# Row maxima of an attention block in two bf16 parts, stacked by two transfers of one partition each

## The reference

```python
x = x + layernorm(attn(layernorm(x), wq, wk, wv, wo))
x = x + layernorm(ffn(layernorm(x), W_base, b_base, W_gate, A, B))

# attn
scores = einsum('bqhd,bkhd->bhqk', q, k) / sqrt(HEAD_DIM)     # q, k after rotary embedding
scores = scores + mask                                        # causal
attn = softmax(scores, axis=-1)
out = einsum('bhqk,bkhd->bqhd', attn, v).reshape(bsz, seq_len, 512)
return out @ wo
```

## Time and profile before

| | us |
|---|---|
| three runs: median | 265.6 |
| lowest, highest | 265.14, 267.56 |
| profiled execution, its own time | 264.58 |
| its span, first to last instruction | 262.9 |
| mean granted clock of TensorE | 0.95 of 2.4 GHz |
| busy: TensorE matmul | 208.9 |
| busy: VectorE | 173.1 |
| busy: ScalarE | 136.1 |
| busy: POOL | 117.8 |

### The profile page before, as it was taken

The page is one execution under the profiler, slowest core; times in us unless marked ns, Lnnn a source line. Parts: engine busy times, 40 slices in busy tenths (PEclk is TensorE's granted clock), DMA queues, the critical chain, the costliest instruction groups (busy, mean ns, idle before and its releaser), DMA issues.

```text
span 262.9 us, 3819 instructions
## 1 busy us (share of the span) xinstructions
PE 208.9 (79%) x1291; PEld 128.0 (49%) x1304; DVE 173.1 (66%) x414; ACT 136.1 (52%) x238; POOL 117.8 (45%) x93
## 2 busy tenths in 40 slices
PE   0799999876764999959994999699479888997860
PEld 0666534343432544434541544144379667886750
DVE  1974257776958567726773673346178988988874
ACT  2432503330343767747845664673085384778672
POOL 8001425522293666736827533881544253222132
PEclk9999999999998699968999799999979999999995
DMA  6993379779920607749066304033420001101113
GB/s 201 368 385 146 104 209 216 236 258 193 280 73 4 150 6 244 152 84 191 12 125 115 82 9 87 1 62 71 82 55 30 2 0 41 40 2 40 40 41 120
DMA packets 33962, 29.95 MB, mean 114 GB/s; under 512 B 3736, under 2 KB 29464, under 8 KB 33944
## 3 DMA queue, kind: packets, MB, share of 16 engines
q1 hardware_dynamic: 33944, 29.72, 42.4%
HBM read 17.19 MB, written 10.09 MB: 104 GB/s over the span
## 4 chain that ended last, share of the span: by engine, by line
PE 26%; DVE 18%; SPq 17%; DMA 16%; issue 11%; POOL 5%; ACT 4%; POOLq 1%; DVEq 0%; ACTq 0%
DMA region_b<-mrow 7%; SPq L364 5%; SPq L366 4%; PE ps L1082 4%; DVE stats L739 3%; PE ps L997 3%; PE ps L1056 3%; PE ps L973 3%; SPq L308 3%; PE ps L987 3%; DMA region_b<-q_scr 2%; DMA rden_bc<-r_scr 2%; PE ps L1145 2%; SPq L324 2%; POOL region_b L495 2%
## 5 line engine op out<-in xcount | busy, mean ns | idle before, releaser
L913 DVE TENSOR_REDUCE nmax<-ps 128x4 f32<-128x1024 f32 x32 | 39.1, 1223 | 25.7 <-PE ps L1056 25.7
L508 POOL TENSOR_SCALAR_AFFINE_SELECT region_a<-region_a 128x1024 f32<-128x1024 f32 x32 | 35.2, 1108 | 24.5 <-ACT region_a L685 24.4
L1082 PE MATMUL ps<-region_b,kst 99*128 99x512 bf16 x96 | 30.0, 420 | 10.5 <-DMA region_b<-mrow 9.2
L685 ACT ACTIVATE region_a<-ps 128x1024 f32<-128x1024 f32 x32 | 32.7, 1021 | 1.9 <-PE ps L1082 1.9
L682 ACT ACTIVATE region_a<-ps 128x512 f32<-128x512 f32 x32 | 19.2, 598 | 22.0 <-PE ps L1082 21.4
L987 PE MATMUL ps<-region_a,region_c 128*128 128x512 f32 x64 | 29.0, 598 | 0.0
L910 DVE TENSOR_REDUCE nmax<-ps 128x4 f32<-128x512 f32 x32 | 21.8, 683 | 9.4 <-PE ps L1040 9.3
L1097 PE MATMUL ps<-region_a,v_aug 128*32 128x512 f32 x192 | 25.2, 603 | 1.7 <-POOL region_a L508 1.7
L550 ACT ACTIVATE std<-mv,eps_sb 128x1 f32<-128x1 f32 x32 | 9.4, 293 | 32.6 <-DVE mv L740 32.6
L1056 PEld LDWEIGHTS ps<-kst,region_b 96*128 96x128 bf16 x256 | 18.9, 105 | 7.8 <-issue 2.8
L544 ACT ACT_TABLE_LOAD x17 | 21.8, 1283 | 1.1 <-PEq L1242 0.8
(11 more groups left out here) (107 smaller groups left out, 422.7 us busy)
## 6 DMA issues: line engine op xcount, KB each, us to landing
region_b<-q_scr SPq DMA_DIRECT2D x8, 768.0 KB, 6.9
q_scr<-region_c SPq DMA_DIRECT2D x8, 384.0 KB, 3.5
x_sb<-x SPq DMA_DIRECT2D x8, 256.0 KB, 5.4
q_scr<-region_c SPq DMA_DIRECT2D x8, 256.0 KB, 3.4
attn_t<-o_sb SPq DMA_DIRECT2D x32, 64.0 KB, 2.3
rden_bc<-r_scr SPq DMA_DIRECT2D x8, 256.0 KB, 3.3
out<-region_b SPq DMA_DIRECT2D x8, 256.0 KB, 2.0
kst<-k_scr SPq DMA_DIRECT2D x8, 192.0 KB, 3.3
```

The costliest lines, as they stand in the source:

```text
L508: pool.affine_select(out=blocks, in_=blocks, compare_op=ALU.is_ge, fill=0.0, base=0, pattern=[[0, 2], [0, REP], [1, P]], channel_multiplie ...
L685: nc.scalar.activation(probs[:, u % PRING, 1:3, :], ps[:, 4:6, :], ACT.Exp, scale=float(HEAD_DIM) ** -0.5).then_inc(exp_done, 1)
L913: nc.vector.tensor_reduce(nmax[:, gi % 2, 1, heads], ps[:, 1:3, :].rearrange("p a (r k) -> p r a k", r=REP), AX.XY, ALU.max, negate=True). ...
L1082: last = nc.tensor.matmul(ps[:, 3 + j, :], kst[0:TROWS, slot, k, kt * P:(kt + 1) * P], qst[0:TROWS, slot, k * REP:(k + 1) * REP, qt * P:(q ...
```

## The change

The maxima go in two bf16 parts: a cast to bf16, and a subtraction whose result is written as bf16. The third part, its cast and its subtraction are left out, and with them the tile `nmax_r`. The contraction of L1082 has 98 rows where it had 99. The stack is issued as two transfers, each from 16 partitions of `mrow` to one partition of `qst`; both add to the same semaphore, and the waits for it count 32 per group where they counted 16. In the new file the stack's issue is L353, the cast L925 and the subtraction L926; the lines of SP behind it are two further down.

```diff
+MAX_PARTS = 2
...
-TROWS = SROWS + PARTS
+TROWS = SROWS + MAX_PARTS
...
-        nmax_r = sb("nmax_r", [P, 2, 2, GROUP_HEADS])
-        nmax_p = sb("nmax_p", [P, 2, PARTS, GROUP_HEADS], BF16)
+        nmax_p = sb("nmax_p", [P, 2, MAX_PARTS, GROUP_HEADS], BF16)
...
             def stack_max(gi):
                 sp.wait_ge(mrow_ready, gi + 1)
-                sp.dma_start(qst[SROWS:TROWS, gi % RING, :, :], mrow[0:PARTS * GROUP_HEADS, gi % 2, :])\
-                    .then_inc(mrow_stacked[gi % 2], 16)
+                for part in range(MAX_PARTS):
+                    sp.dma_start(qst[SROWS + part:SROWS + part + 1, gi % RING, :, :],
+                                 mrow[part * GROUP_HEADS:(part + 1) * GROUP_HEADS, gi % 2, :])\
+                        .then_inc(mrow_stacked[gi % 2], 16)
...
                     if gi >= 2:
-                        act.wait_ge(mrow_stacked[gi % 2], 16 * (gi // 2))
-                    nc.scalar.copy(mrow[0:PARTS * GROUP_HEADS, gi % 2, :],
-                                   ps[0:PARTS * GROUP_HEADS, 0, 0:P].bitcast(BF16)).then_inc(mrow_ready, 1)
+                        act.wait_ge(mrow_stacked[gi % 2], 16 * MAX_PARTS * (gi // 2))
+                    nc.scalar.copy(mrow[0:MAX_PARTS * GROUP_HEADS, gi % 2, :],
+                                   ps[0:MAX_PARTS * GROUP_HEADS, 0, 0:P].bitcast(BF16)).then_inc(mrow_ready, 1)
...
-                    full, left = nmax[:, (gi - 1) % 2, :, :], nmax_r[:, (gi - 1) % 2, :, :]
-                    high, mid, low = (nmax_p[:, :, j, :] for j in range(PARTS))
+                    full = nmax[:, (gi - 1) % 2, :, :]
+                    high, low = (nmax_p[:, :, j, :] for j in range(MAX_PARTS))
...
                     link(nc.vector.tensor_copy(high, full))
-                    link(nc.vector.tensor_tensor(left, full, high, ALU.subtract))
-                    link(nc.vector.tensor_copy(mid, left))
-                    nc.vector.tensor_tensor(low, left, mid, ALU.subtract).then_inc(nmax_split, 1)
+                    nc.vector.tensor_tensor(low, full, high, ALU.subtract).then_inc(nmax_split, 1)
...
-                    last = nc.tensor.transpose(ps[0:PARTS * GROUP_HEADS, 0, qt * 64:(qt + 1) * 64].bitcast(BF16),
+                    last = nc.tensor.transpose(ps[0:MAX_PARTS * GROUP_HEADS, 0, qt * 64:(qt + 1) * 64].bitcast(BF16),
...
-                    pe.wait_ge(mrow_stacked[gi % 2], 16 * (gi // 2 + 1))
+                    pe.wait_ge(mrow_stacked[gi % 2], 16 * MAX_PARTS * (gi // 2 + 1))
```

## The result

Over 20 executions of each, the changed kernel took 266.00 us in the median (263.30 to 267.13) and the kernel before 265.76 (262.25 to 269.63). The ratio is 1.010, with a 95% interval of 1.0059 to 1.014. Two repetitions gave 1.0024 and 1.0025. So the forecast of 265.8 us is within 0.2 us of both means, but a ratio of 1.010 would put the changed kernel at 268.3.

A forecast was written before the change was run, and what follows sets the result against it. It looked to the attention stage, where the row maxima's stack transfer held 7% of the span, the chain's largest entry. Terms -0.3 + 0.45 - 0.4 + 0.5 = +0.25 us gave 265.8 us by the median, range 263.4 to 267.8.

The forecast's parts named there:

- Part 1: VectorE's split: dropping a cast and a subtraction saves 0.42 us per group, on the path only in group 1; -0.3 us.
- Part 3: The stack's spread over DMA engines, 16 instead of 3, shifts its landing: -0.4 us in group 3, +0.5 in group 5.
- Part 2: SP's queue: one more stack issue per group, counting only in group 2 ahead of the writes and send_out; +0.45 us.
- Part 3, group 3: Spread over the engines, the stack lands right behind the load ahead, at about 114.1 instead of 114.48; -0.4 us.
- Part 3, group 5: The stack must now wait for a lagging engine too, landing at 143.8 instead of 143.25; +0.5 us.
- The first: Rival: TensorE's clock does not fall in group 1, worth about 2 us, giving 263.8 us; chance 0.14.
- The second: Rival: no engine lags in group 5, the stack lands with the load at 142.7, giving 264.8 us; chance 0.17.
- third: Rival: the transfer is not spread, each one-partition destination uses one engine, issues cost 0.75 us; 266.9 us, chance 0.08.
- The fourth: Rival: a longer TensorE stall behind group 5's stack brings another half-clock stretch, up to 1.6 us; 267.4 us, chance 0.16.

The follow-up runs named there:

- one transfer: The changed kernel's two parts, but each stack issued as a single transfer to two partitions; ratios to the kernel before 0.9898, 0.9838 and 0.9862, mean 262.54 us.
- the third pair: Third runs, on the same chip, of the changed kernel (266.07 us) and of its version with a single two-partition stack transfer (262.86 us).
- the second profile of the kernel before: Profile from running the kernel before against itself, with no edit; 266.02 against 265.03 us, ratio 1.0008.
- the one-transfer kernel with the long split: Two parts, each stack as a single transfer, with an unused subtraction and cast added to VectorE's split; 263.58 us, ratio 0.9913 to the kernel before.

## Why the prediction was right or wrong

The mean came out near the forecast by luck, since the errors of the terms have opposite signs. The steps that failed are Part 1, where a gain of about 1.1 us was put at 0.3, and Part 3, where group 3 was to gain 0.4 us and lost about 0.3, and group 5 was to lose 0.5 and lost about 0.1. The 1.0% of the first comparison is not explained by any term: it did not come back in two repetitions, and the intervals of those reach from 0.9986 to 1.0065.

**Part 1, the split, -0.3: wrong, mis-sized.** The step reads "two operations remain in the new code at the same two places, so I leave these long ones in". It took 1.22 and 1.03 us as properties of the places. They were waits for GpSimd, and which operations meet it depends on where each falls; with half as many, none beyond 0.60 us was left in this profile. Putting the two operations back cost 0.9 and 1.4 us by the means, and the run from the copy of group 0 to that of group 2 is 1.2 us shorter without them, so the term is about -1.1, to within some 0.5. In sight of the rows shown this could have been known: two identical operations with 0.19 and 1.03 us need a reason.

**Part 2, the second issue, +0.45 in group 2: right as far as it goes, too narrow.** L353 takes 0.59 us in the median, as the den_pk issue; in group 2 the run to the load became 0.4, 0.7 and 0.6 us longer in the three profiles of the changed kernel. But I allowed the cost in one group. The experiment with an issue that TensorE does not wait for lost 2.0 us against one transfer. In the third pair the lag of two transfers, counted from the first issue in group 2, is 0.7 us at the load of group 3, 0.9 at its stack, 1.5 at the load of group 5 (38.96 against 37.45) and 2.1 at its stack. So a second 0.6 us is lost between the group-3 stack and the next load, where I had written 0: not by SP, whose run of issues up to that load is as long in both (6.94 and 6.97 us), but by TensorE's first scores at 1.2 GHz.

**Part 3, group 3, -0.4: wrong.** The stack lands 0.3 to 0.4 us behind the load, where it had landed 0.5 behind; the gain is 0.1 to 0.2, and from the load's issue on (6.58 us before; 6.90, 7.03 and 6.83 now) more than that is lost: the term is about +0.3. The second issue, put at 0 here since the load is still draining, moves the end of the stack all the same.

**Part 3, group 5, +0.5: the mechanism as forecast, the size not.** The stack, 0.45 us before the load's end with three engines, is 0.3 to 0.4 after it in the three profiles of the changed kernel; with one transfer of two partitions it is 0.5 to 0.6 before again. That fits a transfer that lies on all engines and ends only with the last of them. But the load now lands 7.4 to 7.7 us after its issue, where it took 8.2 and 8.4, so the stack ends 7.73, 8.07 and 8.01 us after that issue, against 7.73 and 7.93 before: the term is about +0.1. Against one transfer (7.40 and 7.42) it is +0.5.

**The rivals.** The first (no slow stretch in group 1) happened in the profile (the row 82.20:89.00 is at 0.99), but only since the stretch came some 7 us earlier; the second profile of the kernel before has it there too (74.8 to 81.7), so it moves between executions of one kernel. The second and third did not happen: the stack landed behind the load, the transfers lay on 16 engines each, and the issues took 0.59 us. The fourth, another slow stretch behind a longer stall, has support in the total, but not at its place. Behind the stack of group 5 the stretch is 6.8, 3.4 and 3.4 us long in the three profiles of the changed kernel and 3.4 and 6.8 in the two of the kernel before. What all three of the changed kernel have and the two before have not is one of some 3.5 us between 168.8 and 174.6 us. The mean granted clock over the executions is 0.940 for the changed kernel (44) and 0.948 for the one before (116 that list it). Within the kernel before, executions at a clock of 0.9375 or lower averaged 268.8 us (18), those above 0.9535 263.8 (29); between 0.9375 and 0.9445 the kernel before has 266.9 (15) and the changed one 265.8 (26). So at an equal clock the change gains about a microsecond, and its lower clock gives about that back. That the longer stalls (13.3 us against 10.7) lower the clock was not tried by itself.

**The sum** was +0.25 = -0.3 + 0.45 - 0.4 + 0.5; measured is -0.1 on the means, and the same four terms read from the profiles are about -1.1 + 0.6 + 0.3 + 0.1 = -0.1. Taken by the experiments it is -1.1 (split), about -2 that comes with the smaller stack, and +3.1 (second transfer). The -2 stays partly open: the one-transfer kernel with the long split runs all four operations and still beats the kernel before by 0.9% [0.9859, 0.9967]. It differs from it only in the 32 packets instead of 48 and an issue of 0.65 to 0.69 us instead of 0.74 to 0.79, and in TensorE's 98 rows for 99; which of these does it was not separated. Its mean clock is 0.9545 against 0.9481, which by the line above is worth 1.2 us, so by that estimate only 0.6 of its 1.8 us is left. What the prediction lacked most was this variant: I costed the diff as one piece and never asked what one transfer of two parts would give.

## What to carry to other kernels

Cost both halves of a change by themselves: here the shorter split and the narrower payload won some 3 us and the second transfer lost them again, and the total looked like a change that does nothing. Where a small operation of VectorE lasts five times as long as its like, as here 1.02 us beside 0.19, look for GpSimd's instruction beside it, count how many such operations stand in a row, and shorten the row before shortening the operation. Here a transfer laid on all engines behind a large load ended 0.3 to 0.4 us behind it, and an issue on the saturated queue cost 0.6 us or more to all that followed, waited for or not. A landing is best counted from the issue of the load and not from its end, which moves too. And where single executions spread over 8 us with the clock, a difference under 1% needs the clock beside every mean.

## What the runs showed of the hardware that was not expected

A cast of 0.17 us on VectorE was held for 3.15 us by three selects of GpSimd that followed one another without a gap, while VectorE's reductions out of PSUM took their usual 0.68 and 1.2 us beside such selects (in the second run of the kernel before at 106.32 and 106.92, with a select from 106.49 to 107.59). In group 5 one transfer with three destination partitions and one with two end ahead of a load issued just before (0.5 to 0.6 us), while two with one partition each come 0.3 to 0.4 behind; in group 3 all of them end 0.2 to 0.5 behind their load. With the group-5 stack from ScalarE's queue, the weight load's wait put down to it was 2.5 us, where it is 4.1 on SP (one transfer in both); the matmul behind it was by then waiting for ScalarE's exponent (2.35 us).
